# Gated attention and a mixture of experts in one program: the mixture's opening stands in attention's last five tiles, and the first keys are fetched beside the gates

## The reference, cut to what matters

```python
# cell, per head of 32 numbers; 16 heads
log_D = (cumsum(log_sigmoid(fg)) differences, lower triangle) + ig
D = exp(log_D - max(log_D));  C = (q @ k.T / sqrt(32)) * D
Cn = C / (max(abs(sum(C)), exp(-max_log_D)) + 1e-6);  h = Cn @ v
hn = (h - mean(h)) * rsqrt(var(h) + 1e-6) * ln_scale
x = x + tanh(g_xattn) * cell(layernorm(x), ctx, ctx)
# mixture
logits = layernorm(x) @ gate_w.T;  scores = sqrt(softplus(logits))
idx = top_k(scores + gate_b, 2);  w = scores[idx] / sum
out_e = (silu(xe @ W1.T) * (xe @ W3.T)) @ W2.T      # 352 hidden, at most 256 tokens each
x = x + tanh(g_ffn) * (sum_k w_k * out_(idx_k) + shared(layernorm(x)))
```

## Time and profile before

| | |
|---|---|
| time, median of 3 runs | 800.07 us (797.6 to 801.73) |
| profiled execution | 800.37 us, its span 798.6 us |
| instructions | 20254 |
| PE busy | 693.0 us (87%) |
| VectorE busy | 504.8 us (63%) |
| ScalarE busy | 411.1 us (51%) |
| GpSimd busy | 390.0 us (49%) |
| mean granted PE clock | 0.953 |
| DMA | 135.57 MB, mean 170 GB/s |

### The profile page before, as it was taken

How to read it: one execution, slowest core, us unless ns; L and a number is a source line. 1 busy time by engine, 2 the same in 40 slices (tenths; PEclk the granted TensorE clock), 3 DMA queues, 4 the chain that set the end, 5 groups by cost and what they waited for, 6 DMA issues and landing times.

```text
span 798.6 us, 20254 instructions
## 1 busy us (share of the span) xinstructions
PE 693.0 (87%) x7407; PEld 603.7 (76%) x7408; DVE 504.8 (63%) x992; ACT 411.1 (51%) x848; POOL 390.0 (49%) x594
## 2 busy tenths in 40 slices
PE   0876079999999993799999999999999999999994
PEld 0553057777777772588889998999999999999993
DVE  4762837777777776876437888433666667676750
ACT  0667246666666763554445233222556666666662
POOL 2110347888888885321112425123237575757654
PEclk9989559999999997799999999999999999999998
DMA  7883274644545411477763222233478888888954
GB/s 251 276 268 99 89 209 146 186 127 157 162 132 178 139 65 56 166 256 279 250 193 99 84 79 65 95 93 108 158 237 208 246 233 252 225 257 218 257 135 56
DMA packets 90720, 135.57 MB, mean 170 GB/s; under 512 B 16720, under 2 KB 44112, under 8 KB 90672
## 3 DMA queue, kind: packets, MB, share of 16 engines
q1 hardware_dynamic: 74128, 107.41, 41.3%
q0 software_dynamic: 7168, 17.04, 10.7%
q10 hardware_dynamic: 9376, 10.49, 4.1%
HBM read 92.32 MB, written 34.21 MB: 158 GB/s over the span
## 4 chain that ended last, share of the span: by engine, by line
PE 52%; DVE 4%; DMA 1%; POOL 1%; ACT 1%; issue 1%; POOLq 0%; ACTq 0%; DVEq 0%
PE psH L1206 32%; PE psY L1224 15%; PE psR L1251 2%; PE psT L1186 2%; DMA out<-ystage,sidx 1%; PE psT L1259 1%; POOL out L1713 1%; DVE xnorm L1624 1%; PE psG L1266 1%; DVE xl L1445 1%; DVE stats L1515 1%; DVE over13h L1624 1%; DVE w13l L1457 0%; ACT over13l L1393 0%; DVE over2l L1615 0%
## 5 line engine op out<-in xcount | busy, mean ns | idle before, releaser
L1206 PE MATMUL psH<-xh,w13h 128*128 128x256 f32 (+1 forms) x768 | 222.6, 290 | 3.0 <-DVE w13l L1457 3.0
L1206 PE MATMUL psH<-xh,w13l 128*128 128x256 f32 (+1 forms) x768 | 216.6, 282 | 0.0
L1206 PE MATMUL psH<-xl,w13h 128*128 128x256 f32 (+1 forms) x768 | 215.9, 281 | 0.0
L1681 POOL TENSOR_TENSOR hl<-sg,hh 128x256 fp32r<-128x256 f32 (+1 forms) x96 | 78.5, 825 | 207.1 <-ACT hh L1325 206.3
L1206 PEld LDWEIGHTS psH<-xh,w13h 128*128 128x128 f32 (+1 forms) x768 | 138.5, 180 | 12.0 <-issue 7.4
L1206 PEld LDWEIGHTS psH<-xl,w13h 128*128 128x128 f32 (+1 forms) x768 | 138.9, 181 | 0.7
L1206 PEld LDWEIGHTS psH<-xh,w13l 128*128 128x128 f32 (+1 forms) x768 | 138.8, 181 | 0.0
L1320 ACT ACTIVATE sg<-psH 128x256 f32<-128x256 f32 (+1 forms) x96 | 36.5, 380 | 130.4 <-PE psH L1206 125.5
L1451 DVE TENSOR_TENSOR sg<-sg,psH 128x256 f32<-128x256 f32 (+1 forms) x96 | 40.0, 417 | 97.6 <-ACT sg L1320 97.5
L731 ACT ACTIVATE dec<-ring 128x512 f32<-128x512 f32 x128 | 74.2, 591 | 28.2 <-PE ring L636 27.7
L807 DVE SCALAR_TENSOR_TENSOR dec<-psQ,dec 128x512 f32<-128x512 f32 x128 | 79.4, 681 | 8.8 <-PE psQ L648 7.8
(11 more groups left out here) (224 smaller groups left out, 1397.8 us busy)
## 6 DMA issues: line engine op xcount, KB each, us to landing
raw<-w13T SPq DMA_DIRECT2D x64, 352.0 KB, 5.3
gcT<-ctxT ACTq DMA_DIRECT2D x8, 1024.0 KB, 6.8
kT<-ctxT SPq DMA_DIRECT2D x16, 512.0 KB, 5.2
ctxs<-ctx SPq DMA_DIRECT2D x16, 512.0 KB, 3.5
xn<-xnorm SPq DMA_DIRECT2D x16, 512.0 KB, 4.0
out<-xres SPq DMA_DIRECT2D x16, 512.0 KB
raw<-w2T SPq DMA_DIRECT2D x16, 512.0 KB
qst<-qT_all SPq DMA_DIRECT2D x14, 512.0 KB, 6.1
```

What stands on the lines that cost most here:

```text
L1206: last = nc.tensor.matmul(psH[m][0:n, v, :], w[wp][:, c, col:col + n], x[xp][:, c, :], start=(c == 0 and k == 0), stop=(c == DC - 1 and k ...
L1681: nc.gpsimd.tensor_tensor(hs[u.p][1][0:n, m, :], sg[0:n, m, :], hs[u.p][0][0:n, m, :].bitcast(F32), ALU.subtract).then_inc(hl_ready, 1)
```

## The change

1. Attention and mixture become one block. Each stage now returns five functions, one per engine; the mixture's are generators, which run up to the next `yield` when attention's function calls `next(more)`. The barrier between the stages is gone. Buffers and psum banks are laid out so that what the opening writes is free by then; PE waits before psH until the ring banks are emptied, and before the first psY for the last take.
2. The loop of attention has six rounds, and tiles 27 to 30 are written out behind it. After a step n of VectorE, n = 27 to 31: two pieces; two pieces; two weight quarters; two pieces and a quarter; two pieces, a quarter and both `split_x`. Two further calls of four pieces each stand after take(31) and residual(30). Order of the pieces: measure(0) 4, norm(0) 4, measure(1) 4, measure(2) 4, norm(1) 4 and so on. ScalarE: quarters 0 and 1 after step 28, 2 after 29, 3 after 30; copy of t=0 after keep_output(31), copy of t=1 and both `split_x` after root(30), table load and w2 after root(31). PE: turn t=0 after values(31), t=1 after back(31). GpSimd: the first root after step 29, the second after variance(31), the third and w2's low part last. SP: the weights' 7 transfers after the decay rows of batch 13.
3. After the walk's slot 0 VectorE gets 2 pieces and not 6.
4. The first keys and the first context are loaded by SP in the gates' stage, behind the gate rows, into buffers that live from there on; attention's SP then loads decay rows, `em`, decay rows, context 1.

The diff, cut (buffer layout, names and the plain rewrite of blocks into functions are left out):

```diff
@@ gate_stage, sync
             for k in range(2):
                 sp.dma_start(head[:, k, :, :], ...).then_inc(head_in[k], 16)
+            sp.dma_start(g.kT0[:, :, :], d.ctxT[0].rearrange("(c p) t -> p c t", p=P)).then_inc(g.kT_in[0], 16)
+            sp.dma_start(g.ctx0[:, :, :], d.ctx[0].rearrange("(c p) d -> p c d", p=P)).then_inc(g.ctx_in[0], 16)
@@ attention_stage
-        R0, RPL, LOOPS = 3, 4, 7
+        R0, RPL, LOOPS = 3, 4, 6
...
-            step(LOOPS, R0, True)
-            drain(LOOPS, R0)
+            for r in range(R0, R0 + RPL):
+                step(LOOPS, r, False)
+                late(RPL * LOOPS + r)
+            step(LOOPS + 1, R0, True)
+            late(NT - 1)
...
             load_decay(0, 0)
             load_keys(0, 0)
-            load_ctx(0, 0)
+            load_em(0)
             load_decay(0, 1)
-            load_em(0)
             load_ctx(1, 1)
...
+                if b == B - 3:
+                    sp.wait_ge(q_in[0], 16 * (B // 2 - 2))
+                    sp.wait_ge(q_in[1], 16 * (B // 2 - 2))
+                    next(more)
+            list(more)
@@ tensor
+            values(i, r, bank(r, OUT + 1))
+            next(more)
+            back(i, r, uses(i, r, OUT + 1))
+            list(more)
@@ scalar
+            run(act, c_, 4, step, lambda n: next(more) if n in (NT - 4, NT - 3, NT - 2) else None)
+            keep_output(uses(i, r, OUT + 1), bank(r, OUT + 1))
+            next(more)
+            root(i, r - 1)
+            next(more)
+            square(i, r)
+            root(i, r)
+            list(more)
@@ vector
+            run(dve, c_, 4, step, lambda n: next(more))
+            take(i, r)
+            next(more)
+            residual(i, r - 1)
+            next(more)
+            residual(i, r)
+            list(more)
@@ gpsimd
+            run(pool, c_, 4 * 6, step, lambda n: next(more) if n == NT - 3 else None)
+            normalise(i, r - 1)
+            variance(i, r)
+            next(more)
+            normalise(i, r)
+            list(more)
@@ mixture_stage, tensor
-            side.issue(-1, 2)
+            side.issue(-1, 1)
+            yield
+            side.issue(-1, 1)
+            pe.wait_ge(g.ring_emptied, g.ring_uses)
@@ scalar
+            for pieces in ((0, 1), (2,), (3,)):
+                for n in pieces:
+                    split0(n)
+                yield
+            side.issue(-1, 1)
+            yield
+            side.issue(-1, 1)
+            for j in range(2):
+                split_x(early(0), j)
+            yield
             nc.scalar.preload_act_table_set("silu_and_others")
-            for j in range(2):
-                side.issue(-1, 1)
-                split_x(early(0), j)
-            for n in range(DC + 2):
+            for n in range(DC, DC + 2):
                 split0(n)
@@ vector
                 yield from measure(0)
-                for p in range(B // 2):
+                yield from norm(0)
+                yield from measure(1)
+                for p in range(1, B // 2):
...
-            side.issue(-1, 12)
-            for j in range(2):
-                split_x(early(0), j)
-            split13(early(0))
-            walk(dve, step, side, lambda slot: 6 if slot == 0 else 2 if slot < AT_LOGITS else 1)
+            for count, quarters in ((2, ()), (2, ()), (0, (0, 1)), (2, (2,)), (2, (3,))):
+                side.issue(-1, count)
+                split13(early(0), quarters)
+                if quarters == (3,):
+                    for j in range(2):
+                        split_x(early(0), j)
+                yield
+            for _ in range(2):
+                side.issue(-1, 4)
+                yield
+            walk(dve, step, side, lambda slot: 2 if slot < AT_LOGITS else 1)
@@ gpsimd
-                    yield 4 * p - 1
+                    yield 4 * p - 5
...
-            side.issue(-1, 2)
+            side.issue(-1, 1)
+            yield
+            side.issue(-1, 1)
+            yield
+            side.issue(-1, 1)
```

More of the change, by code:

```diff
@@ L553, in uses, with run @@
             return USES * i + FIRST[r] + j
-        def run(eng, chain_obj, per, step, drain):
+        def run(eng, chain_obj, per, step, late):
             for r in range(R0):
@@ L712, in step @@
                     decay(i, r + 1, 1, bank(r, next2(r) + 1))
[L714 to L718, removed]
             for k in range(2):
@@ L848, in step, with gpsimd @@
                     residual(i, r - 2)
[L850 to L857, removed]
+            run(dve, c_, 4, step, lambda n: next(more))
+            i, r = LAST
+            take(i, r)
[4 more added lines that the diff above has]
+            list(more)
+        def gpsimd(pool, more):
             c_ = Chain(pool, pch)
@@ L942, in step @@
                     variance(i, r - 1)
[L944 to L949, removed]
+            run(pool, c_, 4 * 6, step, lambda n: next(more) if n == NT - 3 else None)
+            i, r = LAST
+            normalise(i, r - 1)
[3 more added lines that the diff above has]
+            list(more)
+        return sync, tensor, scalar, vector, gpsimd
 def shared_pieces(raw13, raw2, w13, w2):
@@ L1451, in gated, with split13 @@
                 nc.vector.tensor_tensor(sg[0:n, m, :], sg[0:n, m, :], psH[m][0:n, 1, :], ALU.mult).then_inc(hh_done, 1)
-            def split13(u):
+            def split13(u, quarters=range(DC)):
                 h, l = w13[u.slot]
-                for k in range(DC):
+                for k in quarters:
                     dve.wait_ge(wh13, DC * u.wset + k + 1)
@@ L1821, in build, with _ @@
                 gate_stage(nc, g, d)
-            attention_stage(nc, g, d)
-        mixture_stage(nc, g, d)
+            attention = attention_stage(nc, g, d, stages)
+        mixture = mixture_stage(nc, g, d, stages)
+        with stages:
+            block = stages.enter_context(nc.Block())
+            first, then = [dict(zip(("sync", "tensor", "scalar", "vector", "gpsimd"), s)) for s in (attention, mixture)]
+            @block.sync
+            def _(sync):
+                first["sync"](sync, then["sync"](sync))
+            @block.tensor
+            def _(pe):
+                first["tensor"](pe, then["tensor"](pe))
+            @block.scalar
+            def _(act):
+                first["scalar"](act, then["scalar"](act))
+            @block.vector
+            def _(dve):
+                first["vector"](dve, then["vector"](dve))
+            @block.gpsimd
+            def _(pool):
+                first["gpsimd"](pool, then["gpsimd"](pool))
 def kernel(**inputs):
```

133 lines of the change are left out of this document (68 added, 65 removed).

## The result

| | before | changed |
|---|---|---|
| time, median | 800.07 us (797.6 to 801.73) | 793.82 us (790.37 to 794.53) |
| profiled execution | 800.37 us, span 798.6 | 790.37 us, span 788.6 |
| mean granted PE clock | 0.953 | 0.973 |
| turn of router tile 4 | 335.93 us | 323.83 us |
| first `psY` | 362.05 us | 353.08 us |

The ratio is 0.9921, 95% interval 0.9902 to 0.994: 6.3 us less. The forecast was 788.7, which is 5.1 too little, with 793.8 inside the range of 785 to 794.5. The profiled execution is the quickest of the five of the changed kernel, so its gain of 10.0 us is not that of the median. Both the profile's own gain and the rest have to be accounted for.

A forecast was written before the change was run, and what follows sets the result against it. TensorE's single line of work was taken as the bound, with a hole near 310 us to fill. 800.4 less 10.9 at the fifth router turn, less 0.5 at attention's start, gave 789.0; less 0.3 for the median, 788.7 us; range 785 to 794.5.

The forecast's parts named there:

- The late tiles: Attention's last five tiles: of 6.5 us added VectorE work 3.6 lies on the path; weigh(31) ends at 308.1, not 304.01.
- meetings: VectorE and GpSimd slowing each other in attention's late tiles, three new cases: 0.5 us taken, bounds 0 and 1.7.
- The walk: Step-by-step recurrence through tiles 28 to 31 with the unchanged tiles' times: weigh(29) ends at 293.57, weigh(31) 3.6 us later.
- From weigh(31) to the first `psH`: Attention's end into the mixture: drain of 2.9 us as before, then copies and splits; psH at 315.5, not 327.50.
- From `psH` to turn 4: Mixture's opening: 9.4 us of VectorE work from 315.5 puts the fifth router turn at 325.0; PE stalls 1.5 to 3.
- The start: Attention's beginning: keys fetched during the gates let queries(0) start 0.5 us earlier, bounds 0 and 1.5.
- After turn 4: Rest of the mixture: VectorE's slots and PE's load stay as before, so the 10.9 us gain carries to the end.
- the DMA term: Shared weights ahead of batch 14's keys: decay rows land at 275.5 to 277.5, slack 0 to 2; cost 0, bound 2.
- rival (c): TensorE's clock falls to its lower level at PE's pauses in late attention and the opening: 801 to 809, say 806; chance 0.04.
- Rival (a): Late attention: all VectorE's added work on the path, meetings at 1.7, decay rows 2 us late: 794.5; chance 0.13.
- rival (b): VectorE's added work in late attention hides, 1.9 on the path, and attention's start gives 1.5: 785.5; chance 0.09.
- (d): At 316 us something other than rows and weights holds PE, so the 16 us hole at most halves: 796; chance 0.04.

The follow-up runs named there:

- the second profile: The changed kernel measured again without any edit, for another profile: median 793.65 us, ratio 0.9910 to the kernel before; its profiled execution took 796.46 us.
- keys in attention: Against the changed kernel, the first keys and context are loaded in attention again and not during the gates: median 794.89 us, ratio 0.9941 to the kernel before.
- loads later: Against the changed kernel, SP issues the 2.1 MB of shared weights behind batch 14's decay rows: median 791.79 us, ratio 0.9903 to the kernel before.

## Why the prediction was right in direction and 5 us too good

By its own steps, in the profiled execution first:

- *The late tiles*: forecast +4.1 at weigh(31) (3.6 of pieces, 0.5 of meetings). From queries(27) on they were 4.5 longer: 0.5 more of wait in front of the decay row, 4.0 the rest. Taking the pieces out gave 3.6 back, and the 0.4 left stayed when they were out. (The walk adds up to 293.46 and not 293.57 at weigh(29), so its 3.6 is 3.5.) The places are right but for one: queries(30) and values(31) wait, while queries(29), forecast 0.56 later, don't (6.52 behind 28 as before). By the prediction's own sign, over 7 us in the last five tiles, the second profile would have spoken against it: 10.7 there, with the clock down.
- *From weigh(31) to the first `psH`*: forecast 7.4, measured 8.9. The drain was taken as before at the upper clock; with the clock down at 306 it was 4.5 and not 2.9 up to `back`. This is the step that failed there: the granted clock was said to stay at 1.00 up to 312. Three other profiles in which the clock holds there (the changed kernel again, keys in attention, loads later) have 7.4, the forecast.
- *From `psH` to turn 4*: forecast 9.5, measured 9.3, with PE stalled 1.5 for ScalarE's copy (behind the table load and the split of `w2`) and 1.07 for the norm; 1.5 to 3 was forecast for the norm. That this stall swallows the price of the lower clock is shown by the run with the pieces behind attention.
- *The start*: forecast 0.5, bound 1.5 if the clock rises with it. It was over the bound, 1.9: 0.4 for the queries, and 1.5 more up to queries(2), with the clock up earlier. Another 1.0 us of the profiled execution's lead was there before the keys are wanted, in the norms' stage, which the change leaves alone.
- *After turn 4*: "PE is as busy as before; I carry 10.9 to the end". This is the largest mistake of the profiled execution: 29.3 us to the first `psY` and not 26.1. Moving GpSimd's low part alone gave 2.5 of the 3.1 back. The port meetings were looked for in attention, at 0.5, and not in the stretch behind, where a 4.08 us piece of GpSimd stands beside VectorE now that both run ahead of PE.

The sum: 789.0, less 1.0 and 1.4 at the start, plus 0.4, 1.5, less 0.2, plus 3.1, less 1.1 between the first `psY` and the end is 790.3, the 790.4 of the profiled execution within rounding. The last term can't be laid to the change: that stretch is 435.5 us here, 436.6 before and 436.5 in the second profile. That the forecast of 789.0 is only 1.4 off is in part luck: 5.0 us of cost that it didn't have stand against 3.7 us of gain that it didn't have either, 2.1 of which can't be laid to the change.

The other 3.4 us, up to the median, I put down to the DMA term and to the clock. Slack 0 to 2 was worked out from 10.7 us of transfer, and a wait of 0 taken; the wait was 1.06 to 3.00 in eight profiles, in six of them 1.5 to 1.9. The 289 GB/s was about right (347 from 264 to 270, 296 from 270 to 274, 237 to 276). SP was 0.3 and 0.6 us late with the pair (issued at 266.58 and 267.12; the earlier trace rows less the 2.9 by which queries(27) are earlier gives 266.3 and 266.6), and the bytes in front were more than the 3.1 MB of the prediction: 0.5 MB of context, issued at 260.54, had landed only at 264.10, 2.3 us behind the issue of the first weights. PE had the row at 275.3, on the time scale of the kernel before 278.2, where 275.5 to 277.5 was forecast. So the estimate of the landing was too early, and of the slack drawn from it the favourable end was taken. Behind this wait the clock fell in half of the profiles, and in some again behind the waits for weigh. That is rival (c) in a mild form: it was priced as all or nothing, 806 or 0, with "a fall at tile 30 costs 5 and stays a gain" as an aside. How often it falls in executions without a profile wasn't measured by rows; their mean clocks, 0.962 to 0.973 over both sets of runs of the changed kernel, go with the times (790.0 at 0.971, 795.1 at 0.964). With the loads later, the medians were 1.9 and 2.0 lower in two comparisons, neither of them clear of the intervals alone. So the mechanism is shown in the profiles, its share in the median is argued, and some 1.4 of the 3.4 us stay open; falls of the clock behind the waits for weigh are the likely rest.

Rival (a), 794.5, comes nearest to the median, and only in part for its own reasons: the pieces were not all on the path (3.6 of 6.5), the decay rows were the 2 late. Of rival (b) the part on the start came true, but the late tiles did pay; (d) is out, for PE's waits in the hole fell by more than half, 16.4 to 7.3 us.

The Trainium skill, SBUF — State Buffer, "SBUF: two separate sides", calls the port pair an exclusive lock for a whole instruction, which VectorE takes for an operation with two SBUF inputs or in a two-port mode. Weighed in the prediction at 0.5 us, it is what the runs bear out most plainly: 2.62 against 0.68 for the split, 2.39, 3.04 and 3.17 against 1.00 for two norms, each time with `w2l` beside it, and the split ends about its own length behind the first `w2l`. The norms have one tensor input, so by the page's words they would have to run in a two-port mode, which no row here names.

## What to carry to other kernels

When work is moved into a stage so that two engines run ahead of the third, look for the long instructions of GpSimd that now stand beside VectorE's, also behind the stretch that was changed, and put them where VectorE has slack; here that was worth 2.5 us in the profile and 3.4 between medians whose intervals touch, on top of the change's 6. Put added work behind the steps that have room, not behind the last ones, and put bulk loads behind the small rows that the matrix engine will want next: a slack that works out to between 0 and 2 us, with nothing counted for what is already in the queue, is to be booked as a wait. And price a short wait of TensorE with a chance of the clock's fall behind it: here it came behind four of eight and five of twelve.

## What was not expected of the hardware

- Behind a wait of PE of 1.5 to 3 us for the decay row, in a stretch in which it is busy at 0.9 otherwise, the clock was at its lower level in four of eight profiles; behind 1.06, 1.56, 1.58 and 1.68 us it stayed at 1.00. The prediction had priced a fall there at a chance of 0.04.
- Without the wait of 0.5 or 1.0 us for the keys, the upper clock came 2.0 to 3.5 us behind the start of queries(0) in eight of ten profiles, and 8.0 and 8.2 in the two others; with it, 9.1 and 9.8 in the two profiles that have it. The early rise made the next two tiles 1.5 us shorter.
- One program's executions differ by 6 us in this way (790.4 and 796.5), and the tiles from queries(27) to weigh(31) alone by 6.2 (34.9 and 41.1).
